# Softmax denominators: four 32-column sums, one small reciprocal, and three DMAs in place of eight wide reciprocals

## The reference

```python
latent_kv = x @ w_kv_down
kv = latent_kv @ w_kv_up                       # k and v, 16 heads of 64 each
q = (x @ w_q).reshape(Bx, Tx, N_HEAD, HEAD_SIZE)
att = jnp.einsum('bqhd,bkhd->bhqk', q, k) * HEAD_SIZE ** (-0.5)
att = jnp.where(causal, att, -jnp.inf)
att = jax.nn.softmax(att, axis=-1)             # exp(att - max) / sum: the sum is the denominator
y = jnp.einsum('bhqk,bkhd->bqhd', att, v).reshape(Bx, Tx, HD)
return y @ w_out                               # added to x
```

## Time and profile before

| | |
|---|---|
| timed runs | 2334.26 us median of 3 (2328.85 to 2338.5) |
| profiled execution | 2332.32 us, its span 2330.9 us |
| busy in the span | PE 2098.8 us (90%), DVE 1517.2 (65%), POOL 1429.6 (61%), ACT 1115.0 (48%) |
| granted TensorE clock, mean | 0.963 |
| DMA | 19.67 MB, 2.4% of the 16 engines' time in the program's queue |

### The profile page before, as it was taken

How to read it: one execution, slowest core, us unless ns; L and a number is a source line. 1 busy time by engine, 2 the same in 40 slices (tenths; PEclk the granted TensorE clock), 3 DMA queues, 4 the chain that set the end, 5 groups by cost and what they waited for, 6 DMA issues and landing times.

```text
span 2330.9 us, 35003 instructions
## 1 busy us (share of the span) xinstructions
PE 2098.8 (90%) x12848; PEld 1280.5 (55%) x12848; DVE 1517.2 (65%) x3154; ACT 1115.0 (48%) x2223; POOL 1429.6 (61%) x816
## 2 busy tenths in 40 slices
PE   5997678999999999999899999998999999999889
PEld 3665445655555555555555555554555555555456
DVE  5788456676767676767565767676757675767243
ACT  4776433444444444444454444444444444444475
POOL 1333215766777767677656667676677777767812
PEclk9998789999999999999999999999999999999989
DMA  3000000000000000000000000000000000000001
GB/s 104 1 1 1 9 7 1 8 2 7 1 8 1 8 1 8 1 8 1 8 1 8 1 8 1 8 1 7 1 8 1 8 1 8 1 1 1 1 32 55
DMA packets 12216, 19.67 MB, mean 8 GB/s; under 512 B 1168, under 2 KB 9488, under 8 KB 12048
## 3 DMA queue, kind: packets, MB, share of 16 engines
q1 hardware_dynamic: 12048, 17.44, 2.4%
HBM read 13.24 MB, written 4.19 MB: 7 GB/s over the span
## 4 chain that ended last, share of the span: by engine, by line
PE 58%; DVE 21%; ACT 8%; POOL 6%; issue 6%; DMA 0%; ACTq 0%; POOLq 0%; DVEq 0%
PE heads_out L779 17%; PE beside L598 13%; PE two_heads L738 6%; DVE part_max L967 4%; PE scores L761 3%; PE scores L767 3%; PE scores L763 3%; PE scores L765 3%; DVE rden L992 3%; POOL acc L1249 3%; PE scores L598 2%; PE beside L788 2%; ACT prob L1165 2%; DVE two_heads L964 2%; DVE stats L816 2%
## 5 line engine op out<-in xcount | busy, mean ns | idle before, releaser
L1249 POOL TENSOR_TENSOR acc<-acc,prob 128x1024 f32<-128x1024 f32 (+3 forms) x512 | 1016.2, 1985 | 236.4 <-ACT prob L1165 177.3
L1165 ACT ACTIVATE prob<-scores 128x512 f32<-128x512 f32 (+3 forms) x1280 | 579.7, 539 | 641.1 <-PE scores L767 271.2
L967 DVE TENSOR_REDUCE part_max<-two_heads 128x2 f32<-128x1024 f32 x384 | 467.4, 1217 | 236.5 <-PE two_heads L738 234.9
L779 PE MATMUL heads_out<-prob,V 128*64 128x512 f32 (+3 forms) x2560 | 560.3, 560 | 1.7 <-ACT prob L1165 1.6
L738 PE MATMUL two_heads<-k_hi,q_hi 64*128 64x512 f32 (+3 forms) x1280 | 281.1, 434 | 101.4 <-DVE part_max L964 63.9
L964 DVE CUSTOM_DVE_ANT_0 two_heads<-two_heads,mask 128x128 f32<-128x128 f32 (+3 forms) x512 | 241.4, 513 | 105.9 <-PE two_heads L738 105.8
L779 PEld LDWEIGHTS heads_out<-prob,V 128*64 128x64 f32 x2560 | 159.3, 139 | 238.8 <-issue 213.0
L738 PEld LDWEIGHTS two_heads<-k_hi,q_hi 64*128 64x128 f32 x1280 | 121.2, 185 | 297.8 <-issue 124.6
L992 DVE RECIPROCAL rden<-rden 128x64 f32<-128x64 f32 x512 | 260.4, 531 | 20.7 <-ACT rden L1176 20.7
L761 PE MATMUL scores<-q_hi,k_hi 64*128 64x512 f32 (+3 forms) x1280 | 235.8, 363 | 0.8 <-ACT neg_max L1152 0.8
L763 PE MATMUL scores<-q_hi,k_lo 64*128 64x512 f32 (+3 forms) x1280 | 235.9, 362 | 0.0
(11 more groups left out here) (299 smaller groups left out, 3081.7 us busy)
## 6 DMA issues: line engine op xcount, KB each, us to landing
wP_raw<-wPair SPq DMA_DIRECT2D x16, 384.0 KB, 3.0
X<-u SPq DMA_DIRECT2D x8, 512.0 KB, 9.0
out<-X SPq DMA_DIRECT2D x8, 512.0 KB, 2.9
wA_sb<-wA SPq DMA_DIRECT2D x1, 768.0 KB, 7.4
wFa<-wF SPq DMA_DIRECT2D x1, 768.0 KB, 7.7
wFb<-wF SPq DMA_DIRECT2D x1, 768.0 KB, 4.2
gamma_beta<-gb SPq DMA_DIRECT2D x1, 256.0 KB, 4.3
prob<-wKD SPq DMA_DIRECT2D x1, 128.0 KB, 2.1
```

Source lines behind the costliest of these rows:

```text
L779: made = pe.matmul(heads_out[head(h), x0:], V[(idx - j + c) % NVS][:, tt, head(h)], prob[step % NPROB][:, h, x0:], start=t == 0, stop=t == ...
L967: made = ve.reduce_max(part_max[:, t, :, c:c + 1], two_heads[:, :, 0:width], AX.X)
L1165: ac.activation(prob[step % NPROB][:, h, x0:], bank(task, h)[:, x0:], ACT.Exp).then_inc(empty(task, h)[0], 1)
L1249: po.tensor_tensor(total[:, :, x0:], total[:, :, x0:], new[:, :, x0:], ALU.add).then_inc(acc_ok, 1)
```

## The change

After it, `denominators` lets PE multiply 32 columns of ones four times: head h and half e of the query rows go to partitions 32(2h+e) onwards, 256 columns each. ACT copies 128x256 to `den_rows`. Each sum is now there in 32 equal rows, and SP takes one row of each of the four and lays them out as `den`, 16 partitions of 64. DVE inverts that once. SP writes it to `rden_rows` in DRAM (2 x 512), waits until it is there, and reads each head's row into 64 partitions of `rden`. POOL's multiplication waits for that. The tail gets fixed distances: `denominators` not before the step index s+2 of the round list, `invert` s+6, `scale_out` s+8, `two_parts` s+10, where s is the round in which the unit's last step is weighed (a round is 2 steps); of the fillers, the two projection halves get due steps one apart.

```diff
 NKS, NVS = 7, 6
 LEAD = 20
+NDEN, QUAD = 8, 32
 MIX = [(1, 0), (1, 1), (0, 0), (0, 1)]
...
-        def invert():
+            chore()
+
+        def chore():
             if self.chores:
                 self.chore(self.chores[0])
-            else:
-                for _ in range(2 if UNITS[divisor or 0][2] in (0, 3) else 1):
-                    if pieces:
-                        self.need("invert", divisor, pieces.pop(0))
 
...
-        def output():
-
-            nonlocal divisor
-            if parts and (not parts[0] or ("project", parts[0] - 1, 1) in self.done):
-                idx = parts.pop(0)
-                self.need("two_parts", idx)
-                fillers.extend([(s + 2, s + 4, ("project", idx, half)) for half in range(2)])
-            if divisor is not None and not pieces:
-                self.need("scale_out", divisor)
-                parts.append(divisor)
-                divisor = None
-            if divisor is None and ended and ended[0][0] <= s:
-                divisor = ended.pop(0)[1]
-                self.need("denominators", divisor)
-                pieces.extend(range(2 * TPB))
-                return True
-            return False
+        def output(idx):
+
+            later.extend([(s + 2, ("denominators", idx)), (s + 6, ("invert", idx)), (s + 8, ("scale_out", idx)), (s + 10, ("two_parts", idx))])
+
+        def due(kind):
+
+            ready = [x for x in later if x[1][0] == kind and x[0] <= s]
+            if not ready or kind == "two_parts" and ready[0][1][1] and ("project", ready[0][1][1] - 1, 1) not in self.done:
+                return False
+            later.remove(ready[0])
+            self.need(*ready[0][1])
+            if kind == "two_parts":
+                fillers.extend([(s + 2, s + 4 + half, ("project", ready[0][1][1], half)) for half in range(2)])
+            return True
 
...
             if at < goal:
                 maximum()
+            due("invert")
             for step in steps[s:s + 2]:
                 self.need("score", *step)
             if at < goal:
                 maximum()
             else:
-                invert()
+                chore()
             filler(10 ** 6)
...
                     self.need("take_out", idx)
-                    ended.append((s + 2, idx))
+                    output(idx)
             if at < goal:
                 maximum()
-            if not output():
+            due("two_parts")
+            due("scale_out")
+            if not due("denominators"):
                 filler(s + 8)
...
+    rden_rows = nc.dram_tensor("rden_rows", (2, BLK), F32).ap()
...
-            ones = sb(ph, "ones", [P, DH])
+            ones = sb(ph, "ones", [P, QUAD])
...
+            den_rows = sb(ph, "den_rows", [P, BLK // 2])
+            den = sb(ph, "den", [2 * NDEN, BLK // NDEN])
+            inverse = sb(ph, "inverse", [2 * NDEN, BLK // NDEN])
...
                     for h in range(2):
-                        made = pe.matmul(bank(task)[head(h), :], ones[:, :], acc[idx % 2][:, h, :], start=True, stop=True)
+                        for e in range(2):
+                            rows, half = slice((2 * h + e) * QUAD, (2 * h + e + 1) * QUAD), slice(e * BLK // 2, (e + 1) * BLK // 2)
+                            made = pe.matmul(bank(task)[rows, 0:BLK // 2], ones[:, :], acc[idx % 2][:, h, half], start=True, stop=True, tile_position=(0, rows.start))
...
                 elif kind == "invert":
-                    _, idx, i = task
-                    cols = slice(i * DH, (i + 1) * DH)
-                    w.wait_ge(*empty(("denominators", idx)))
-                    ve.reciprocal(rden[:, cols], rden[:, cols]).then_inc(inverted, 1)
+                    idx = task[1]
+                    w.wait_ge(den_spread, 16 * (idx + 1))
+                    w.wait_ge(rden_out, 16 * idx)
+                    ve.reciprocal(inverse[:, :], den[:, :]).then_inc(inverted, 1)
...
-                    w.wait_ge(oT_ok, idx)
-                    ac.activation(rden[:, :], bank(task), ACT.Copy).then_inc(empty(task)[0], 1)
+                    w.wait_ge(den_spread, 16 * idx)
+                    ac.activation(den_rows[:, :], bank(task)[:, 0:BLK // 2], ACT.Copy).then_inc(empty(task)[0], 1)
...
-                    w.wait_ge(inverted, 2 * TPB * (idx + 1))
+                    w.wait_ge(rden_in, 32 * (idx + 1))
                     po.tensor_tensor(oT[idx % 2][:, :], oT[idx % 2][:, :], rden[:, :], ALU.mult).then_inc(oT_ok, 1)
...
+                elif kind == "denominators":
+                    idx = task[1]
+                    w.wait_ge(*empty(task))
+                    w.wait_ge(inverted, idx)
+                    sp.dma_start(den[:, :], den_rows[0:P:QUAD, :]).then_inc(den_spread, 16)
+                elif kind == "invert":
+                    idx = task[1]
+                    w.wait_ge(inverted, idx + 1)
+                    w.wait_ge(rden_in, 32 * idx)
+                    sp.dma_start(rden_rows.rearrange("h (c x) -> (h c) x", c=NDEN), inverse[:, :]).then_inc(rden_out, 16)
+                    w.wait_ge(rden_out, 16 * (idx + 1))
+                    w.wait_ge(oT_ok, idx)
+                    for h in range(2):
+                        sp.dma_start(rden[head(h), :], rden_rows[h:h + 1, :].broadcast_to([DH, BLK])).then_inc(rden_in, 16)
                 elif kind == "load_pair" and task[1]:
```

18 lines of the change are left out of this document (9 added, 9 removed).

## The result

The changed kernel takes 2264.47 us (median of 4 runs, 2264.23 to 2265.47), the kernel before, measured beside it, 2334.35 us (2328.85 to 2338.5). The ratio is 0.970, with an interval of 0.968 to 0.972: 70 us less, 3.0%. The profiled execution took 2264.5 us, its span 2263.2.

A forecast was written before the change was run, and what follows sets the result against it. The prediction took TensorE to set the pace, VectorE counting only where TensorE waits for it. Reciprocals -22, matmuls -16 and end of attention +3 gave -35, so 2332.3 became 2297 us; 8-in-10 range 2281 to 2336.

The forecast's parts named there:

- What is late next: TensorE's other stops for maxima, up to 2.2 us, have no reciprocal before them; no gain was counted there.
- Reciprocals, -22: One small reciprocal per unit instead of eight: 16 us from the wait for `X`, 6.4 from short-unit waits for maxima.
- R2: Rival, 13%: the reciprocals were already covered by the TensorE-VectorE ping-pong and the matmul gains half; 2322 to 2332 us.
- Matmuls, -16: Denominator sums: four 32-column tiles run together, 0.86 to 0.55 us per unit, 20 us over 64 units, partly handed back.
- Four fifths: Share of the sums' 20 us counted as gain, since some is handed back in TensorE's waits: 16 us.
- Order, 0: Projection comes one round earlier for units of 8 and 12 steps; same work, so 0.
- Copy, DMAs, weight load, 0 each: ScalarE's smaller copy, denominator transfers and the later weight load cost 0; weight load barely hidden, bound +15 us.
- R4: Rival, 9%: weight load or denominators' way back 2 us or more late at ScalarE or GpSimd; 2337 us.
- End of attention, +3: After the last unit nothing hides the denominators' DMA way: 7.7 us instead of 4.1, sums shorter; bounds 0 and +6.
- Clock, 0 within 5: Granted clock in the attention stage: nothing counted either way, with 5 us as bound on both sides.

The follow-up runs named there:

- before_no_split: Kernel before, without VectorE's subtraction for the output weights' low part from the third pair of heads on: 2299.1 us, 36.8 less.
- before_lo12: Kernel before, with the output weights' high and low parts made one round earlier, nothing left out: 2308.5 us, 27.5 less.
- before_lo8: Kernel before, with the output weights' high and low parts made one round later, nothing left out: 2301.9 us, 34.1 less.
- sums_only: Kernel before, with only its two 64-column sum matmuls replaced by the four 32-column ones: 2296.0 us, 40.7 less.
- old_load: Changed kernel with the two old sum matmuls and seven wide reciprocals per unit on a scratch tile put back: 2313.0 us, 23.7 less than before.
- one_recip: Kernel before, with seven of the eight 128x64 reciprocals of each unit left out: 2306.4 us, 30.3 less.
- den_j0: Changed kernel with the short first units' denominators and what follows them one round later, nothing left out: 2253.7 us, ratio to before 0.965.
- no_dma: Changed kernel without the small denominator DMAs of every unit but the first: 2256.3 us, 8.2 under the changed kernel.

## Why the prediction was wrong, by its steps

- **The missing term, -28.** "What is late next: PE's other stops for maxima (up to 2.2 us) have no reciprocal in the run of DVE work before them." The statement holds at 1012.71 above, and the conclusion that they stay was wrong. I looked in those runs for what the change removes, not for what set their length. It was an instruction that waited for GpSimd, so its length hung on its start, and every shift of TensorE against GpSimd could change it. before_no_split (37 us), before_lo12 and before_lo8 (28 and 34), sums_only and old_load show it. Counted with the forecast it gives 2297 - 28 = 2269 us, so this is the step that put the time below the range.
- **Reciprocals, -22.** In the right order, 3 to 8 us too small: 25 us of waits and 30 us of time by one_recip. `X` was sized nearly right (12.9 of 16.0 us there, 9.9 in the changed kernel), and so were the unmasked maxima (7.1 for 6.4, though only 4.0 in the changed kernel); the wait for `neg_max` (5.3 us) was not counted. R2 (covered) is out. VectorE's busy time fell to 1320, not 1290: I took off 0.51 us for each of 448 reciprocals, but their records overlap their neighbours', and one_recip, which leaves out just these, is 175 us less busy, 0.39 each.
- **Matmuls, -16.** Right: four tiles together. The forecast saved 0.31 us per unit, measured is 0.96 - 0.57 - 0.09 = 0.30, 19 us. "Four fifths" was not needed, nothing was handed back. The estimate from the Trainium skill ("TensorE: Matmul & The Clock Gate", "Measured speedup vs the span model", 2.38x for three column tiles) would have made it 9. The measured 0.57 us less some 0.1 for the layout change behind the sums (the prediction's figure, not measured apart) is 0.47, between the 0.54 by the page's share and my 0.43.
- **Order, 0.** Wrong by about 11: I followed the projection's and the weight load's moves, and the short units' sums, one round earlier, were in no term. They came behind the key products on the one spare bank (den_j0). I listed no wait for that bank.
- **Copy, DMAs, weight load, 0 each.** Right. POOL waited 9.3 us in total for the spread 15 times and 8.4 in the last unit, and TensorE did not feel the first; no_dma leaves them some 2 us. VectorE's two waits for `den` (12.2 us) are both in the last two units. No wait of ACT for the weight load shows up, so R4 is out (its price there should read 15 x 2.5 = 37.5, not 40).
- **End of attention, +3.** Right: from ACT's copy of the sums (2141.18) to the first normalised tile behind attention (2155.70) it takes 14.5 us; before it was 2212.09 to 2223.33, 11.2.
- **Clock, 0 within 5.** At or beyond its bound: the changed kernel's four executions have 160 us at the low level, the kernel before 172 in its profile and 175 to 182 in the later sets, 5 to 9 us by the estimate above.

The sum as measured: -28 (subtraction) - 30 (reciprocals) - 19 (sums) + 11 (`k_lo`) + 3 (tail) = -63, and with 5 to 9 for the clock -68 to -72, against the -70. The terms were measured in different kernels, each to a few us, so that the sum comes out this well is in part luck. The range failed for the same reason as the time. I held that hardly anything could lie below the forecast's own end, with no rival in which something the change does not touch gets faster; and of the signs listed for being wrong, none could have shown this.

## What to carry to other kernels

Before a small change in a kernel where VectorE and GpSimd both work on SBUF, list VectorE's two-input instructions whose duration varies (here 0.42 to 2.62 us for one shape) and see which of them TensorE waits behind. Their price changes with any shift in time, in either direction, and moving one by a round in the order is a one-number experiment that was worth some 28 us here. In the changed kernel the same move won nothing one round earlier and lost 10 us one round later, so the row's length alone does not tell; the waits behind it do. A speed-up of such a kernel is therefore tested with the old load in the new order and the new load in the old order before it is put down to the load. Where a step moves to another round, look also at what held its PSUM bank just before: 16 sums one round too early cost 11 us.

## What the runs showed that was not expected

- GpSimd waits in the same way when it comes second: in sums_only the subtraction began at 995.08, GpSimd's addition at 995.11, and the addition took 2.64 us instead of 2.37, while the subtraction took its usual 0.43.

```profile
995.08 0.43 DVE L938 TENSOR_TENSOR wP_lo<-wP_raw,wP_hi 128x256 fp32r<-128x256 f32 x1 [2.46 <-ACT wP_hi L1107]
```

```profile
992.56 2.37 POOL L1251 TENSOR_TENSOR acc<-acc,prob 128x1024 f32<-128x1024 f32 x1 [0.17 <-POOL acc L1251]
995.11 2.64 POOL L1251 TENSOR_TENSOR acc<-acc,prob 128x1024 f32<-128x1024 f32 x1 [0.17 <-POOL acc L1251]
```

- A small DMA from SBUF to DRAM (4 KB, 16 rows) landed in 1.4 us and the spread over 64 partitions in 2.9 us; 256 of these small transfers raised the queue's share of the DMA engines from 2.4% to 4.9% and slowed no weight load (3.1 us, before 3.0). The queue's row (packets, MB, share) and the issues (KB each, median us to landing):

```profile
q1 hardware_dynamic: 25616, 34.76, 4.9%
```

```profile
wP_raw<-wPair SPq DMA_DIRECT2D x16, 384.0 KB, 3.1
...
rden<-rden_rows SPq DMA_DIRECT2D x128, 128.0 KB, 2.9
...
rden_rows<-inverse SPq DMA_DIRECT2D x64, 4.0 KB, 1.4
```
